# Stationary y blocks interleaved in pairs, and the split weight rows moved to one phase modulo 256 bytes

## What is computed

```python
W = weights[condition]                                  # (64, 64, 64)
y = einsum('bct,bcd->bdt', x, W)
gate_logits = einsum('bsd,ed->bse', y, gate_w)
top, selected = top_k(gate_logits, 2)
w_full = sum(one_hot(selected, 8) * softmax(top)[..., None], axis=2)
low = einsum('bsd,erd->ebsr', y, lora_A)
out = x + einsum('bsd,od->bso', y, base_w) + base_b \
        + 2.0 * einsum('ebsr,eor,bse->bso', low, lora_B, w_full)
```

## Time and profile before

| | |
|---|---|
| median of three runs | 494.29 us (494.03 to 494.37) |
| the profiled execution | 494.55 us, its span 492.5 us |
| TensorE matmuls | 487.7 us busy, 2771 of them |
| TensorE weight loads | 480.8 us busy, 2771 |
| VectorE | 371.0 us busy |
| ScalarE | 382.2 us busy |
| GpSimd | 128.5 us busy |
| DMA | 43.89 MB, mean 89 GB/s |
| TensorE's granted clock | 1.00 of full speed |

### The profile page before, as it was taken

One profiled execution on the slowest core, in us unless ns is written; L12 is line 12 of the kernel. 1 busy time (PEld: TensorE's weight loads), 2 busy tenths in 40 slices (PEclk: granted clock), 3 DMA queues, 4 the chain that ended last, 5 costly groups with the idle time before them and its releaser, 6 DMA issues.

```text
span 492.5 us, 8737 instructions
## 1 busy us (share of the span) xinstructions
PE 487.7 (99%) x2771; PEld 480.8 (98%) x2771; DVE 371.0 (75%) x800; ACT 382.2 (78%) x740; POOL 128.5 (26%) x111
## 2 busy tenths in 40 slices
PE   8999999999999999999999999999999999999997
PEld 8999999999999999999999999999999999999997
DVE  5988877778787778787787877787877787777653
ACT  4898878878778887788787788887788877887620
POOL 2033202333113333033232223332133320233130
PEclk9999999999999999999999999999999999999999
DMA  8812122221221221221222222212212212211112
GB/s 333 352 43 80 69 91 89 61 95 58 91 91 58 91 96 51 91 92 53 96 63 82 89 79 70 96 53 91 91 55 96 87 59 88 96 53 55 56 43 85
DMA packets 31986, 43.89 MB, mean 89 GB/s; under 512 B 18402, under 2 KB 22498, under 8 KB 31970
## 3 DMA queue, kind: packets, MB, share of 16 engines
q1 hardware_dynamic: 31826, 43.17, 25.0%
q10 hardware_dynamic: 144, 0.52, 0.4%
HBM read 25.00 MB, written 18.68 MB: 89 GB/s over the span
## 4 chain that ended last, share of the span: by engine, by line
PE 91%; DMA 3%; ACT 3%; DVE 1%; SPq 1%; issue 0%; ACTq 0%
PE acc L642 76%; PE acc L674 9%; PE mixed L662 5%; DMA x_sb<-in_x 3%; ACT y_moved L363 1%; ACT x_parts L350 1%; SPq L219 1%; DVE w_raw L467 0%; ACT w_raw L355 0%; DVE w_raw L548 0%; DVE w_raw L551 0%; SPq L215 0%; DVE y_turned L474 0%; DVE y_lo L481 0%; ACT y_hi L386 0%
## 5 line engine op out<-in xcount | busy, mean ns | idle before, releaser
L642 PE MATMUL acc<-w_hi,y_hi 128*128 128x384 f32 (+1 forms) x768 | 257.3, 338 | 0.5 <-ACT w_hi L336 0.3
L642 PE MATMUL acc<-w_lo,y_hi 128*128 128x384 f32 (+1 forms) x768 | 257.0, 338 | 0.0
L642 PE MATMUL acc<-w_hi,y_lo 128*128 128x384 f32 (+1 forms) x768 | 256.6, 337 | 0.0
L363 ACT COPY y_moved<-w_raw 32x256 f32<-32x256 f32 x480 | 194.1, 404 | 38.0 <-DVE w_raw L467 32.3
L295 POOL TENSOR_TENSOR w_raw<-x_sb,bias 128x1024 f32<-128x1024 f32 x32 | 77.2, 2414 | 345.4 <-DVE low L522 277.7
L642 PEld LDWEIGHTS acc<-w_hi,y_hi 128*128 128x128 f32 x768 | 144.0, 188 | 4.0 <-DVE w_raw L548 0.7
L642 PEld LDWEIGHTS acc<-w_lo,y_hi 128*128 128x128 f32 x768 | 143.9, 188 | 2.5
L642 PEld LDWEIGHTS acc<-w_hi,y_lo 128*128 128x128 f32 x768 | 144.0, 188 | 0.0
L467 DVE TENSOR_TENSOR w_raw<-mixed,w_raw 64x1024 f32<-64x1024 f32 x60 | 73.0, 1217 | 30.0 <-ACT w_raw L355 29.6
L474 DVE STREAM_TRANSPOSE y_turned<-y_moved 128x512 f32<-128x512 f32 x60 | 42.3, 706 | 51.2 <-ACT y_moved L363 51.2
L355 ACT COPY w_raw<-mixed 64x1024 f32<-64x1024 f32 x60 | 60.7, 1012 | 20.9 <-PE mixed L662 20.1
(11 more groups left out here) (52 smaller groups left out, 239.7 us busy)
## 6 DMA issues: line engine op xcount, KB each, us to landing
x_sb<-in_x SPq DMA_DIRECT2D x32, 512.0 KB, 3.3
out<-w_raw SPq DMA_DIRECT2D x31, 512.0 KB, 2.6
w_raw<-in_proj_w SPq DMA_DIRECT2D x8, 580.0 KB, 9.5
scratch<-low_squares SPq DMA_DIRECT2D x29, 64.0 KB, 1.5
lowT_raw<-scratch SPq DMA_DIRECT2D x116, 16.0 KB, 1.7
cw<-in_cond_w ACTq DMA_DIRECT2D x1, 512.0 KB, 3.6
lb_raw<-in_lora_b SPq DMA_DIRECT2D x1, 512.0 KB, 16.4
bias<-in_base_b SPq DMA_DIRECT2D x1, 512.0 KB, 17.1
```

The source lines that it names most:

```text
L363: done = nc.scalar.copy(y_moved[q * SQ:(q + 1) * SQ, g, :, :], piece.rearrange("m (k q a) -> m q k a", q=QUARTERS, a=SQ)[:, q, :, :])
L642: return nc.tensor.matmul(acc[:, c % 2, b, 0:hi - lo], y_part[:, c % 2, k, :], w_part[:, k, lo:hi], start=(k == 0 and product == 0), stop= ...
```

## The change

The rows of `w_hi` and `w_lo` become 1216 columns (4864 = 19 x 256 bytes) apart, of which columns 24 to 1183 are used. So every row begins 96 bytes past a multiple of 256. `y_hi` and `y_lo` hold blocks 2 i and 2 i + 1 interleaved column by column: the 128 columns of one block are 8 bytes apart, and blocks of odd k begin 4 bytes past those of even k. `y_turned` becomes one tile of plain blocks, so `turn` writes runs of 32 columns into it, `y_high` reads it as plain runs of 128 and writes with the stride of two elements, and `y_low` reads and writes that stride too. The number, the order and the sizes of the instructions and all waits stay.

```diff
+    PITCH, FIRST = 1216, 24
...
-        w_hi = sb("w_hi", [P, KT, N], F32R)
-        w_lo = sb("w_lo", [P, KT, N], F32R)
+        w_hi_rows = sb("w_hi_rows", [P, KT, PITCH], F32R)
+        w_lo_rows = sb("w_lo_rows", [P, KT, PITCH], F32R)
+        w_hi = w_hi_rows[:, :, FIRST:FIRST + N]
+        w_lo = w_lo_rows[:, :, FIRST:FIRST + N]
...
-        y_turned = sb("y_turned", [P, QUARTERS, KT, SQ], F32)
-        y_hi = sb("y_hi", [P, 2, KT, P], F32R)
-        y_lo = sb("y_lo", [P, 2, KT, P], F32R)
+        y_turned = sb("y_turned", [P, KT, P], F32)
+        y_hi = sb("y_hi", [P, 2, HALF_K, P, 2], F32R)
+        y_lo = sb("y_lo", [P, 2, HALF_K, P, 2], F32R)
...
+        def y_block(part, c, k):
+            return part[:, c % 2, k // 2, :, k % 2]
+        def y_half(part, c, h):
+            return part[:, c % 2, h * HALF_K // 2:(h + 1) * HALF_K // 2].rearrange("p i m e -> p i e m")
         def turned_half(h):
-            return y_turned[:, :, h * HALF_K:(h + 1) * HALF_K, :].rearrange("p g k m -> p k g m")
+            return y_turned[:, h * HALF_K:(h + 1) * HALF_K, :].rearrange("p (i e) m -> p i e m", e=2)
...
             def y_high(j, c, h):
-                high = y_hi[:, c % 2, h * HALF_K:(h + 1) * HALF_K, :].rearrange("p k (g m) -> p k g m", m=SQ)
-                nc.scalar.copy(high, turned_half(h)).then_inc(y_hi_ready, 1)
+                nc.scalar.copy(y_half(y_hi, c, h), turned_half(h)).then_inc(y_hi_ready, 1)
...
             def turn(j, c, h):
-                nc.vector.transpose(y_turned[:, :, ks, :], y_moved[:, :, ks, :]).then_inc(turned, 1)
+                nc.vector.transpose(y_turned[:, ks, :].rearrange("p k (g m) -> p g k m", m=SQ), y_moved[:, :, ks, :]) \
+                    .then_inc(turned, 1)
             def y_low(j, c, h):
-                high = y_hi[:, c % 2, ks, :].bitcast(F32).rearrange("p k (g m) -> p k g m", m=SQ)
-                low_part = y_lo[:, c % 2, ks, :].rearrange("p k (g m) -> p k g m", m=SQ)
-                nc.vector.tensor_tensor(low_part, turned_half(h), high, ALU.subtract).then_inc(y_ready, 1)
+                nc.vector.tensor_tensor(y_half(y_lo, c, h), turned_half(h), y_half(y_hi, c, h).bitcast(F32),
+                                        ALU.subtract).then_inc(y_ready, 1)
...
-                return nc.tensor.matmul(acc[:, c % 2, b, 0:hi - lo], y_part[:, c % 2, k, :], w_part[:, k, lo:hi],
+                return nc.tensor.matmul(acc[:, c % 2, b, 0:hi - lo], y_block(y_part, c, k), w_part[:, k, lo:hi],
```

More of the change, by code:

```diff
@@ L188, in adaln_ffn_kernel, with mixed_half @@
         res_ready = sem("res_ready")
+        def y_block(part, c, k):
+            return part[:, c % 2, k // 2, :, k % 2]
+        def y_half(part, c, h):
+            return part[:, c % 2, h * HALF_K // 2:(h + 1) * HALF_K // 2].rearrange("p i m e -> p i e m")
         def turned_half(h):
-            return y_turned[:, :, h * HALF_K:(h + 1) * HALF_K, :].rearrange("p g k m -> p k g m")
+            return y_turned[:, h * HALF_K:(h + 1) * HALF_K, :].rearrange("p (i e) m -> p i e m", e=2)
+        def mixed_half(h):
+            return mixed[:, h, :].rearrange("p (i e m) -> p i e m", e=2, m=P)
         def lowT_block(c):
@@ L339, in y_high_first @@
                 act.wait_ge(mix_done, 2 * c + h + 1)
-                nc.scalar.copy(y_hi[:, c, h * HALF_K:(h + 1) * HALF_K, :],
-                               mixed[:, h, :].rearrange("p (k m) -> p k m", m=P)).then_inc(y_hi_ready, 1)
+                nc.scalar.copy(y_half(y_hi, c, h), mixed_half(h)).then_inc(y_hi_ready, 1)
             def x_high(j, c, first=False):
@@ L450, in y_low_first @@
                 dve.wait_ge(y_hi_ready, 2 * c + h + 1)
-                ks = slice(h * HALF_K, (h + 1) * HALF_K)
-                nc.vector.tensor_tensor(y_lo[:, c, ks, :], mixed[:, h, :].rearrange("p (k m) -> p k m", m=P),
-                                        y_hi[:, c, ks, :].bitcast(F32), ALU.subtract).then_inc(y_ready, 1)
+                nc.vector.tensor_tensor(y_half(y_lo, c, h), mixed_half(h), y_half(y_hi, c, h).bitcast(F32),
+                                        ALU.subtract).then_inc(y_ready, 1)
             def x_low(j, c, b):
```

## The result

The changed kernel takes 500.51 us (500.01 to 500.63, four runs) against 494.33 us of the kernel before beside it (494.03 to 494.38): a ratio of 1.0124, 95% interval 1.0107 to 1.0142. I had forecast 485.2. The profiled execution has a span of 498.4 us, 5.9 more than before.

A forecast was written before the change was run, and what follows sets the result against it. TensorE's matmul density was taken as the bound. From 494.55 us, 9.1 for the steady steps and 0.4 for the first and last steps gave 485.05, said as 485.2 us; range 483.8 to 508.

The forecast's parts named there:

- What bounds the kernel: Whole kernel: TensorE is busy throughout the 14.97 us steady step, so how densely its matmuls follow each other sets the end.
- The 14.5 ns above the columns: Projection matmuls: 175.6 ns each against 161.1 ns for their columns at 2.4 GHz, 1.04 us a step.
- the column part: Projection matmuls: 0.442 ns a column, 171.0 ns, taken as not removable; reaching it saves 4.6 ns each, 0.33 us a step.
- the experts' 3.5 ns fixed: Expert matmuls of 384 and 256 columns: 3.5 ns of each taken as fixed, beside 0.442 ns a column.
- The bounds: Projection: at best all 14.5 ns a matmul go (-1.04 us a step), at worst they double (+1.04 us).
- Rival (c): Projection: constant distance collides, 3.4 to 14.5 ns more a matmul; 502 to 528 us, middling 507; chance 0.22.
- the slow block k = 3 at 96 bytes: Projection before the change: block k = 3 took 3.4 ns a matmul more than k = 0, a weak sign of address disturbance.
- Rival (b): Projection: load and stream have nothing to do with each other, so nothing changes; within 1 us of 494.3; chance 0.10.
- What is late next: Steady step: VectorE comes next, once its 0.27 us wait at the logits is gone; TensorE then waits for `banks_added`.
- the ring: VectorE's chain from `add_rest` through copies, transposes, `y_low`, bank adds and gates: 14.67 us, holding a step at about 14.68.
- The cap on the gain: Steady steps: at most 8.2 us in 28 steps plus 0.9 us of TensorE running ahead, 9.1 us.
- The y instructions: `y_high`, `y_low` and the transposes on ScalarE and VectorE: other strides, taken to cost 0.

The follow-up runs named there:

- the still stream: The kernel before, with each projection matmul streaming one weight column 384 or 392 times (stride 0) in place of the row: 482.95 us.
- the narrow load: The kernel before, with 32 of the stationary block's 128 columns for k = 1 to 6 of the projection: 494.89 us.

## Why the prediction was wrong

**What bounds the kernel** was right: TensorE fills every step, before and after, and the density of its matmuls sets the end. The 14.5 ns above the columns are there.

**The step that failed** is "I take the column part, 171.0 instead of 175.6 ns: -4.6 ns", the change's only gain. It rested on reading the remainder of 4.6 ns as collisions of load and stream that one constant distance would end. Of the experts' 3.5 ns fixed, which I took for removable, 2.5 stay even when the stream stands still. The column part, 0.442 ns against 0.417 at 2.4 GHz, is the memory rate of 9.0 to 9.1 bytes per ns. What is left for the distance to move is the spread between layouts, 175.5 to 178.3 ns, and before the change the mean was already 175.8, at its lower end. Measured at this term: +2.5 ns a matmul by the spacings (+2.7 against the 175.6 of the step's sum) in place of -4.6.

**The bounds** were -14.5 to +14.5 ns; the lower one is refuted by the rate: at 9.05 bytes per ns the mean of 386.7 columns takes 170.9 ns, with the 2.5 fixed 173.4, some 2 ns below the best layout seen (an estimate).

**Rival (c)** is what happened: a bad constant distance, from the very sign I had named, the slow block k = 3 at 96 bytes. Its smallest price, 502 us, lies 1.5 us above the result. It was read wrongly: 3.4 ns is the block's distance to block k = 0, and over the average of 175.6 it is 2.2 ns, which would have given 499.4 us. That the sign came true is in part luck, since block k = 3 was as slow with all rows at 32 bytes, where the kernel lost nothing. And its mechanism, reads that collide all along, was too strong. I gave it 0.22 because I weighed the idea behind the change above the only row that spoke of this distance. The range, 483.8 to 508, holds the result; the sign and the size of the forecast were wrong. The sum itself gives 485.05; the 0.15 us to the forecast has no term.

**Rival (b)** drew on the Trainium skill, "SBUF — State Buffer": two independent read ports, from which I took that no phase matters. The runs support most of it: with a quarter of the load's columns the matmuls cost as much as with all. But they don't support "nothing": moving rows by 96 bytes costs 4.0 us, and moving y along gives it back.

**What is late next** could be tested with the still stream, where TensorE wants far less. The timeline of VectorE in that kernel:

```profile
199.24 0.42 DVE L551 TENSOR_TENSOR w_raw<-acc,w_raw 128x256 f32<-128x256 f32 x1
199.64 0.17 DVE L489 COPY logits_sb<-acc 128x8 f32<-128x8 f32 x1
...
201.13 1.22 DVE L467 TENSOR_TENSOR w_raw<-mixed,w_raw 64x1024 f32<-64x1024 f32 x1
...
210.71 0.25 DVE L535 TENSOR_TENSOR lowT_lo<-lowT_raw,lowT_hi 128x128 fp32r<-128x128 f32 x1
```

and the waits of TensorE there:

```profile
PE acc L674 <- DVE lowT_lo L535: 7.2, 29, 0.5
```

VectorE's wait at the logits is gone and its steps take 14.55 to 14.66 us, near the 14.68 of the ring. TensorE's new wait, however, is for `lowT_ready` ahead of the experts, 0.25 us on average and up to 0.5 in each of 29 steps, and not for `banks_added` as I wrote, which it waits for once. I had not followed that wait, which is the more pressing. The cap on the gain, 9.1 us in the steady steps, was about right: spacings 12 ns shorter make 0.87 us a step, 24 us in 28 steps, and the kernel gained 11.6 us.

**The y instructions:** `turn` (706 ns, unchanged) and `y_low` (+1 ns) cost nothing, as taken. `y_high` writes with a stride of two elements 47 ns slower, which I took as 0; VectorE's wait still hides it. With rows at offset 0, where both layouts of y have steps of 14.97 to 14.98 us, that wait is 7.4 us in all with plain y and 6.7 with interleaved y: some 25 ns a step of the two `y_high`'s 94 ns.

## What to carry to other kernels

Before a layout is shaped to keep two reads of an engine apart, let each stand still once (a broadcast operand). That takes one execution each and shows which of them holds the engine. A row that speaks of the very value chosen, here block k = 3 at 96 bytes, weighs more than the idea for which it was chosen. But one block among unlike neighbours, good or bad, is no promise of what comes when all take its value.

## What was unexpected of the hardware

- TensorE's stream of float32r goes through SBUF at 9.0 to 9.1 bytes per ns in each partition, less than the 9.6 of one column a cycle. A plain matmul of 384 columns costs 173 to 178 ns on average in these layouts, and 162.5 when the stream stands still. Repeating each column hides it, and a stride of 8 bytes doubles the matmul to 340 ns.
- The Trainium skill, "SBUF — State Buffer" (Specifications (TRN2), the row on cachelines), says that two hits on a 16-byte line suffice for full bandwidth. The stream with columns 8 bytes apart has two hits a line and half the pace, so for this read the measurement decides against it. The weight load with the same stride grew from 188 to 195 ns only, but it fits the same rate (an estimate): the narrow load gives (188 - 108) / 96 = 0.83 ns a column and 81 ns fixed, which leaves 114 ns for the 1024 bytes of the strided one, 9.0 bytes per ns. What size of piece is read at a time isn't told apart by these runs; both 8 and 16 bytes fit. No other stride was run, so the rate per byte walked rests on strides of 0, 4 and 8 bytes.
- In the kernel before, nearly all of the 72 distances in a step stay within 2 ns over the 28 steady steps, whatever the other engines and the DMAs do; three of them are longer in a single step each. Why the distance between the two reads moves it by 1 to 2% while the size of the load doesn't, stays open.
